# Staging two weight matrices of a fused attention and low-rank kernel in DRAM as bf16, and loading their column blocks through the sync queue

## What is computed

```python
xn   = layernorm(x)                                # over the 4096 features
q_c  = rmsnorm(xn @ w_qa, g_qa)                    # w_qa: 4096 x 1536
q    = q_c @ w_qb                                  # 32 heads of 128 + 64
kv   = xn @ w_kva                                  # 4096 x (512 + 64)
k_c, k_rope = kv[..., :512], kv[..., 512:]
k_nope, v   = split(rmsnorm(k_c, g_kva) @ w_kvb)   # 32 heads of 128 + 128
attn = softmax(scale * (q_nope k_nope^T + rope(q_rope) rope(k_rope)^T)) @ v
y    = x + attn @ w_o + xn @ (U * S @ V.T).T       # V: 4096 x 1024
```

## Time and profile before

| | us |
|---|---|
| median of 2 runs | 6011.55 |
| the two runs | 5982.61 and 6040.49 |
| profiled execution | 5879.22 |
| its span, slowest core (core 2) | 5877.2 |
| fastest core | 5810.1 |

### The profile page before, as it was taken

One profiled execution on the slowest core, in us unless ns is written; L12 is line 12 of the kernel. 1 busy time (PEld: TensorE's weight loads), 2 busy tenths in 40 slices (PEclk: granted clock), 3 DMA queues, 4 the chain that ended last, 5 costly groups with the idle time before them and its releaser, 6 DMA issues.

```text
span 5877.2 us, 71732 instructions; the slowest of 8 cores (5810.1 to 5877.2 us)
## 1 busy us (share of the span) xinstructions
PE 4937.0 (84%) x22961; PEld 2153.4 (37%) x23300; DVE 1484.0 (25%) x2367; ACT 2022.7 (34%) x2827; POOL 136.9 (2%) x152
## 2 busy tenths in 40 slices
PE   4777755888888888888888888888888888869999
PEld 1333322333333333333333333333333333334443
DVE  3444445012211222122211221122211221111110
ACT  2333322003344434443454434443444344400000
POOL 0000000000000000000000000000000000000000
PEclk8777766998888988899898988899889989889877
DMA  6222215651000100000000100010000100065561
GB/s 100 44 44 46 42 16 72 64 53 16 6 7 7 12 7 7 7 8 11 7 7 7 12 7 7 7 12 7 7 7 7 12 7 7 1 114 120 119 115 49
DMA packets 217802, 176.48 MB, mean 30 GB/s; under 512 B 138400, under 2 KB 191648, under 8 KB 212208
## 3 DMA queue, kind: packets, MB, share of 16 engines
q0 software_dynamic: 196432, 138.30, 17.1%
q1 hardware_dynamic: 21024, 33.57, 1.9%
HBM read 293.04 MB, written 16.78 MB: 53 GB/s over the span
## 4 chain that ended last, share of the span: by engine, by line
PE 74%; DVE 14%; issue 5%; ACT 4%; DMA 2%; DVEq 1%; ACTq 0%; POOL 0%; POOLq 0%
PE outps L1098 8%; PE sps L961 8%; PE sps L953 8%; PE lps L933 8%; PE avps L940 8%; PE kvps L377 5%; PE sps L814 4%; PE kxps L762 4%; PE sps L804 4%; PE qctps L584 3%; PE kxps L736 2%; DVE bnst L281 2%; PE outps L1109 2%; PE qctps L640 2%; PE sps L889 2%
## 5 line engine op out<-in xcount | busy, mean ns | idle before, releaser
L971 ACT ACTIVATE PT<-sps,bias_col 128x512 bf16<-128x512 f32 x2048 | 1408.3, 688 | 819.3 <-PE sps L961 589.1
L961 PE MATMUL sps<-qropeM,ropeP 65*128 65x512 bf16 x2048 | 846.6, 413 | 47.3 <-DVE mrow L911 40.4
L953 PE MATMUL sps<-qnopeT,knopeT 128*128 128x512 bf16 x1984 | 811.4, 409 | 20.9 <-DVE bias_col L922 15.7
L933 PE MATMUL lps<-PT,ones_bf 128*65 128x512 bf16 x2048 | 816.9, 399 | 1.7
L940 PE MATMUL avps<-PT,V1h 128*128 128x512 bf16 x1920 | 771.7, 402 | 34.0 <-DVE oT L1010 34.0
L1098 PE MATMUL outps<-wo,oT 128*128 128x512 bf16 x1998 | 509.0, 415 | 4.3 <-issue 1.1
L340 PE MATMUL trps<-ident_bf,xn 128*128 128x128 bf16 x1024 | 243.2, 253 | 229.2 <-DVE xnTt L349 138.2
L746 DVE CAST knopeT<-kxps 128x512 bf16<-128x512 f32 x256 | 177.0, 691 | 1020.7 <-PE kxps L736 1009.8
L933 PEld LDWEIGHTS lps<-PT,ones_bf 128*65 128x65 bf16 x2048 | 243.8, 119 | 280.6 <-issue 71.1
L377 PE MATMUL kvps<-w_kva_bf,xnTt 128*128 128x64 bf16 (+1 forms) x2016 | 317.5, 325 | 11.0 <-DVE xnTt L349 10.5
L961 PEld LDWEIGHTS sps<-qropeM,ropeP 65*128 65x128 bf16 x2048 | 211.1, 103 | 312.1 <-issue 109.5
(11 more groups left out here) (127 smaller groups left out, 3680.1 us busy)
## 6 DMA issues: line engine op xcount, KB each, us to landing
xf<-x POOLq DMA_DIRECT2D x32, 1024.0 KB, 9.0
wo<-w_o POOLq DMA_DIRECT2D x8, 4096.0 KB, 34.0
wqb<-w_qb POOLq DMA_DIRECT2D x32, 576.0 KB, 6.7
xres<-x SPq DMA_DIRECT2D x64, 256.0 KB, 3.1
out<-stage SPq DMA_DIRECT2D x64, 256.0 KB, 2.1
wcol<-w_qa POOLq DMA_DIRECT2D x12, 1024.0 KB, 9.9
p2xf<-x POOLq DMA_DIRECT2D x8, 1024.0 KB, 8.3
wcol<-V POOLq DMA_DIRECT2D x8, 1024.0 KB, 9.7
```

Of the source, the lines that this page charges most:

```text
L933: P.op("tensor", lambda e, j=j, sb=sb: e.matmul(l_ps[0:65, :], ones_bf[:, 0:65], PT[sb][:], start=(j == 0), stop=(j == C.KS - 1), skip_gro ...
L953: P.op("tensor", lambda e, ks=ks, sb=sb, qc=qc: e.matmul(s_ps[sb][:], knopeT[:, ks * 128:(ks + 1) * 128], qnopeT[:, qc * 512:qc * 512 + 51 ...
L961: e.matmul(s_ps[sb][:], ropeP[:, ks * 128:(ks + 1) * 128], qropeM[:, qc * 512:qc * 512 + 512], start=False, stop=True),
L971: e.activation(PT[sb][:], s_ps[sb][:], AF.Exp, scale=C.SCALE, bias=bias_col[:]),
```

## The change

Two internal DRAM tensors are added, w_qa_st (4096 x 1536, bf16) and V_st (4096 x 1024, bf16). At the start of stage 1 POOL issues four DMAs from DRAM to DRAM that cast: the first half of w_qa, the first half of V, the second half of w_qa, the second half of V. Each V half waits, on POOL, for the w_qa half before it (same semaphore). They stand in POOL's list after the small constants and before cosT, sinT, w_kva, g_kva and every x tile. In stage 2 the 20 loads of wcol read the bf16 copies, and are issued from SP instead of POOL; their semaphores are qs0 to qs2 instead of qg4, qg5 and qg2. Two start values of waits in stages 2 and 3 that stood for counts of qg2 and qg3 change with them.

```diff
@@ -129,6 +129,8 @@
     out = nc.dram_tensor("out", [C.T_own, C.D], F32, kind="ExternalOutput").ap()
+    w_qa_st = nc.dram_tensor("w_qa_st", [C.D, C.QR], BF16, kind="Internal").ap()
+    V_st = nc.dram_tensor("V_st", [C.D, C.RANK], BF16, kind="Internal").ap()
@@ -202,6 +204,19 @@
             krp_ps = E1(nc.psum_tensor("krpps", [128, 128], F32))
 
+            stg_q = [0, 0]
+            stg_v = [0, 0]
+            for hh in range(2):
+                HD = C.D // 2
+                stg_q[hh] = P.op("gpsimd", lambda e, hh=hh, HD=HD: e.dma_start(
+                    out=w_qa_st[hh * HD:(hh + 1) * HD, :],
+                    in_=w_qa[hh * HD:(hh + 1) * HD, :]),
+                    inc=f"qg{4 + hh}", incn=16)
+                stg_v[hh] = P.op("gpsimd", lambda e, hh=hh, HD=HD: e.dma_start(
+                    out=V_st[hh * HD:(hh + 1) * HD, :],
+                    in_=V[hh * HD:(hh + 1) * HD, :]),
+                    waits=[(f"qg{4 + hh}", stg_q[hh])],
+                    inc=f"qg{4 + hh}", incn=16)
             P.op("gpsimd", cast_dma(cosT_bf[:], cosT[:, :]), inc="qc0", incn=16)
             P.op("gpsimd", cast_dma(sinT_bf[:], sinT[:, :]), inc="qc0", incn=16)
@@ -563,17 +578,19 @@
-            WQ = ["qg4", "qg5", "qg2"]
+            WQ = ["qs0", "qs1", "qs2"]
             NWB = 3 if C.QRC >= 3 else 2
-            wcol_free = [(), (), ()]
-            wcol_free[2] = ((WQ[2], P.c[WQ[2]]),)
+            wcol_free = [
+                ((WQ[0], P.c[WQ[0]]), ("qg4", stg_q[0]), ("qg5", stg_q[1])),
+                ((WQ[1], P.c[WQ[1]]), ("qg4", stg_q[0]), ("qg5", stg_q[1])),
+                ((WQ[2], P.c[WQ[2]]), ("qg4", stg_q[0]), ("qg5", stg_q[1]))]
             for qrc in range(C.QRC):
                 wb = qrc % NWB
-                qw_w = P.op("gpsimd", lambda e, qrc=qrc, wb=wb: e.dma_start(
+                qw_w = P.op("sync", lambda e, qrc=qrc, wb=wb: e.dma_start(
                     out=wcol[wb][:].rearrange("p (c m) -> p c m", c=C.DC),
-                    in_=w_qa[:, qrc * 128:(qrc + 1) * 128].rearrange(
+                    in_=w_qa_st[:, qrc * 128:(qrc + 1) * 128].rearrange(
                         "(c p) m -> p c m", p=128)),
                     waits=wcol_free[wb], inc=WQ[wb], incn=16)
@@ -627,11 +644,14 @@
             for rc in range(C.RC):
                 wb = (C.QRC + rc) % NWB
-                qw_w = P.op("gpsimd", lambda e, rc=rc, wb=wb: e.dma_start(
+                qw_w = P.op("sync", lambda e, rc=rc, wb=wb: e.dma_start(
                     out=wcol[wb][:].rearrange("p (c m) -> p c m", c=C.DC),
-                    in_=V[:, rc * 128:(rc + 1) * 128].rearrange(
+                    in_=V_st[:, rc * 128:(rc + 1) * 128].rearrange(
                         "(c p) m -> p c m", p=128)),
-                    waits=wcol_free[wb], inc=WQ[wb], incn=16)
+                    waits=(list(wcol_free[wb])
+                           + ([("qg4", stg_v[0]), ("qg5", stg_v[1])]
+                              if rc < NWB else [])),
+                    inc=WQ[wb], incn=16)
@@ -691,7 +711,7 @@
-            wkvb_free = [(("qg2", P.c["qg2"]),), (("qg3", P.c["qg3"]),)]
+            wkvb_free = [(), ()]
```

## The result

The change makes the kernel 2.9% slower: the ratio of its time to that of the kernel before is 1.0287, 95% interval 1.0211 to 1.0364. The quickest runs show the step at its cleanest: 6012.15 us after, 5820.09 us before, 192 us or 3.3% apart. The ratio is lower and its interval wide because the kernel before has few runs to compare, and they reach up to 5903.78 us: the mean of six runs after is 6016.30 us, that of 5820.09, 5820.81 and 5903.78 us is 5848.23, and their ratio is 1.0287.

What follows compares the result with a forecast made beforehand. The kernel was taken as bound by matmuls, with transfers nearly all hidden except at the start. Staging 186, POOL waits 6 and stage 2's start 3 gave +195 us on 6011.55, so 6207 us, range 6095 to 6375 us.

Steps and rivals of the forecast that it cites:

- The other signs that I named: Profile after: full DMA share at some 110 GB/s written before statistics near 248 us; stage 2 cycles kept, SP waiting for TensorE.
- The 186: Start of stage 1: us for the four staging DMAs, all exposed, the middle of the traffic price.
- price by reads plus writes: Staging: 62.91 MB of DRAM reads and writes at 314 or 366 GB/s, so 200 or 172 us.
- The waits on POOL: Start of stage 1: V halves waiting for w_qa halves drain the queue, 2 x 3 = 6 us, ends 0 and 10.
- The start of stage 2: wcol loads from SP now run beside p2xf 0 and 1, delaying stage 2 by +3 us, ends -3 and +17.
- the engine price: Staging if only written bytes count: 20.97 MB at 157 or 183 GB/s, 134 or 115 us.
- The wcol loads: Stage 2: nothing waits for the 20 loads, so faster loads are worth 0 us.
- The rival of small pieces that choke SP's queue: Stage 2: 256-byte pieces make wcol loads take twice 9.9 us, about +50 us, 6257 us; chance 0.05.
- The rival that the engines bind: Staging limited by DMA engines, not DRAM: 115 to 134 us, time 6136 to 6155 us; chance 0.14.
- The clock: Rival: longer idle start keeps core 2 at core 0's clock in stage 4, 65 us back, 6142 us; chance 0.05.
- the level: Whole time: 6011.55 + 195 = 6207 us, the median's 132.33 us above the profiled execution assumed unchanged.

Runs made afterwards that it cites:

- the staging hidden in stage 1: The change with staging in 16 pieces behind stage 1's x loads; 5818.96 us beside 5817.6 to 5818.13 of the kernel before, 5827.51 beside 5822.01 to 5837.38.
- four mixes of reads, writes and cast: Head of the queue: the change, then on the kernel before half and full float32 copies and a cast into SBUF; start +192.9, +129.1, +254.1, +123.2 us.
- core 0 alone: The changed kernel with the other seven cores idle; first w_qa half in 32.6 us against 60.0 with eight cores, start at 144.5 us.

## Why the prediction held, point by point

- **Where the cost lies.** I said that all of the staging is exposed because cosT, w_kva and x tile 0 stand behind it, and that nothing else changes. The start moved by 192.9 us, the quickest runs by 192 us, and the staging hidden in stage 1 took the cost away, to within about 1 us. The other signs that I named held too: 109 GB/s written ahead of the statistics, stage 2 as long as before, SP and not POOL waiting for TensorE, and no wait of TensorE for a wcol load.
- **The size.** The sum was 186 + 6 + 3 = +195 us, with the statistics at about 248 us; they start at 246.8 us on core 1. The 186 was the middle of the price by reads plus writes (172 to 200), and the experiments show that this is the right price: 325 to 340 GB/s to a core, in four mixes of reads, writes and cast, against the 314 and 366 that I took from the earlier trace rows. What couldn't be read off the loads, that writes count in the same sum, was chosen and turned out true. That 186 is so close is in part luck: the reason that I gave, eight cores with a full queue, speaks for the 314 GB/s and so for 200 us, not for the middle; the transfer took 189 to 190.
- **The terms within it.** The waits on POOL cost 2.5 to 3.7 us together, not 6; of the 3 us that I put at each, 1 us for the semaphore stood on no row. The start of stage 2 cost 0.3 us as the median of the cores, not +3, and less than one core differs from the next: VectorE waited 9.06 to 14.09 us for the first p2xf before and 8.90 to 13.59 us after, though wcol loads now ran beside it. Two small errors of one sign, which the 186 made up for, since 192.9 - 3.7 leaves 189 us for the transfer.
- **Slips in the working.** The lower end of the range was to be the engine price less half the spread of the two runs shown, but half of 5982.61 to 6040.49 is 29 us and not 40, so it should have been 6107 us and not 6095; nothing hangs on it here. The staged rows written are 3 and 2 KB long and those read 6 and 4 KB, not 3 to 6.
- **The wcol loads.** They land 6.8 us after issue where the earlier trace rows had 9.9 and 9.7, and nobody waited for either. The rival of small pieces that choke SP's queue is wrong: with 256-byte pieces at both ends the loads landed sooner, not later. They also read half the bytes and come from another queue, so this doesn't say what the small pieces cost. The Trainium skill, DMA: Bandwidth & Descriptors, section Specifications, asks for 512 bytes for line rate; no run here has the same loads in larger pieces, and at 6.8 us for 1 MB they were far from being waited for.
- **The rival that the engines bind** is refuted by core 0 alone: it moved 579 GB/s through the same engines.
- **The clock.** I left 5% for a core 2 that would get core 0's clock in stage 4. In the changed kernel's execution core 2's whole mean is 0.870 and no core is below 0.869. But the kernel before has runs of 5817 to 5822 us, too, so its profiled execution of 5879.22 us simply had cores 2 and 3 at 0.79 and 0.80 late in stage 4. Stage 4 of core 2 took 723.7 us there and 655.9 us in the changed kernel, but 655.3 us also in the kernel with the staging hidden, which starts at 53 us as before. So the idle start gave nothing back: the quickest runs of both are still 192 us apart.
- **The step that failed** is the level. I carried the 132.33 us between the profiled execution and the median of two runs over to the new kernel and gave 6207 us. By the ratio, the changed kernel would be at 1.0287 x 6011.55 = 6184 us, which is in my range of 6095 to 6375 us; but the plain median of the changed kernel is 6024.49 us, below it. Those 132 us were not a property of the kernel: the quickest runs of before are 59 us under the profiled execution. The better form of the forecast was the difference, +195 us, on a quick run of the kernel before.

## What to carry to other kernels

What stands ahead of the first tile's load in its queue is paid in full; put there only what the first tile needs, in the order in which it needs it, and put anything that is needed 800 us later behind the loads of a stage that leaves the queue idle. Before making a load cheaper, look at who waits for it: here nobody did, so 20 loads made a third quicker were worth 0 us, whatever they cost to prepare. When a transfer goes from DRAM to DRAM with all cores at work, price it by its reads plus its writes at the rate that the full queue shows in the same kernel.

## What the runs showed of the hardware that I had not expected

A core alone copies and casts from DRAM to DRAM at 579 GB/s of reads plus writes (386 read, 193 written), 1.8 times what it gets beside its neighbour.

The Trainium skill, HBM Reference, section Specifications (TRN2), states about 716 GB/s for the memory of a pair; the pair here reached 630 with two reads to one write and, at 340 for a core with all eight at work, 680 GB/s with reads only, so the measurement stays 5 to 12% under it. The same section also names about 425 GB/s for a core that streams alone, bounded by its DMA engines; this case's copy goes beyond that counted as reads plus writes, and stays under it counted as reads alone (386 GB/s).

An issue from SP isn't always short. The tile wcol in the changed kernel (duration in ns, min/median/max):

```profile
L591 SPq DMA_DIRECT2D wcol<-w_qa_st x12: 359/360/16940, 1045.8 to 1331.8; - x12
```

Most of the twelve issues took 0.36 us. The three at the start of stage 2, one behind the other while the first p2xf loads run, took 2.74, 16.94 and 6.08 us, and on the other seven cores the longest took 15.6 to 17.6 us. SP had nothing else to do. In a kernel whose SP queue also feeds something urgent, this would be a stall. Why it stands there for so long wasn't tried.
